# Graph attention on one core: V of a pair of tiles as seven block products in the scores' banks

## What is computed

```
q, k, v = (heads(x @ W + b) for W, b in the three pairs)      # 16 heads of 32
scores  = q k^T / sqrt(32), -inf where adj == 0
out     = softmax(scores) v  -> (b, s, 512)
x       = layernorm(x + out @ Wo + bo)       # no scale or shift, eps 1e-5
```

## Time and profile before

| | us |
|---|---|
| median of three runs | 822.24 |
| the profiled execution, whole | 821.39 |
| its span, first to last instruction | 819.5 |
| TensorE busy | 812.0 (99%) |
| VectorE busy | 544.9 (66%) |
| GpSimd busy | 512.6 (63%) |
| ScalarE busy | 238.2 (29%) |
| granted TensorE clock, mean | 0.999 |

### The profile page before, as it was taken

The page is one execution under the profiler, slowest core; times in us unless marked ns, Lnnn a source line. Parts: engine busy times, 40 slices in busy tenths (PEclk is TensorE's granted clock), DMA queues, the critical chain, the costliest instruction groups (busy, mean ns, idle before and its releaser), DMA issues.

```text
span 819.5 us, 25422 instructions
## 1 busy us (share of the span) xinstructions
PE 812.0 (99%) x11286; PEld 665.1 (81%) x11286; DVE 544.9 (66%) x691; ACT 238.2 (29%) x315; POOL 512.6 (63%) x407
## 2 busy tenths in 40 slices
PE   9999999999999999999999999999999999999997
PEld 7788888888888888888888888888888888888886
DVE  5667667766567666676665776656766567766795
ACT  6532233221332222332223322133322233223223
POOL 1386667656675565856658566576665767657682
PEclk9999999999999999999999999999999999999999
DMA  9224424253342433424334243352424434234342
GB/s 321 90 79 122 120 81 135 84 143 95 88 143 72 149 92 92 139 70 142 105 91 134 71 144 95 82 154 82 128 88 106 136 82 131 84 108 118 105 105 104
DMA packets 50173, 92.37 MB, mean 113 GB/s; under 512 B 11280, under 2 KB 13328, under 8 KB 47888
## 3 DMA queue, kind: packets, MB, share of 16 engines
q1 hardware_dynamic: 47568, 87.08, 36.2%
q10 hardware_dynamic: 2496, 3.67, 1.6%
HBM read 40.37 MB, written 16.78 MB: 70 GB/s over the span
## 4 chain that ended last, share of the span: by engine, by line
PE 98%; DVE 1%; POOL 0%; ACT 0%; issue 0%; POOLq 0%; DVEq 0%
PE ring L289 23%; PE ring L291 21%; PE ring L290 21%; PE ring L386 7%; PE ring L387 7%; PE ring L390 7%; PE psum_s L357 6%; PE ring L375 6%; PE ring L407 1%; PE ring L309 0%; POOL soft L912 0%; PE ring L313 0%; PE ring L317 0%; DVE soft L717 0%; DVE top L724 0%; ACT soft L568 0%
## 5 line engine op out<-in xcount | busy, mean ns | idle before, releaser
L912 POOL TENSOR_TENSOR soft<-soft,top 128x1024 f32<-128x1024 f32 x62 | 125.2, 2020 | 77.5 <-DVE top L724 77.5
L171 POOL TENSOR_TENSOR soft<-soft,inverse 128x1024 f32<-128x1024 f32 x62 | 118.9, 1918 | 24.9 <-DVE inverse L731 22.2
L563 ACT ACTIVATE kt<-ring,bk 128x512 f32<-128x512 f32 x64 | 43.6, 681 | 258.7 <-PE ring L291 258.6
L889 POOL TENSOR_TENSOR x_lo<-x_raw,x_hi 128x512 fp32r<-128x512 f32 x56 | 72.0, 1286 | 61.1 <-ACT x_hi L548 61.1
L289 PE MATMUL ring<-wv_hi,x_hi 128*128 128x512 f32 x256 | 103.5, 404 | 0.0
L289 PE MATMUL ring<-x_hi,wk_hi 128*128 128x512 f32 x256 | 103.1, 403 | 0.0
L728 DVE TENSOR_REDUCE total<-soft 128x16 f32<-128x1024 f32 x62 | 75.6, 1219 | 41.0 <-ACT soft L568 41.0
L291 PE MATMUL ring<-wv_hi,x_lo 128*128 128x512 f32 x256 | 100.1, 391 | 0.0
L291 PE MATMUL ring<-x_hi,wk_lo 128*128 128x512 f32 x256 | 99.9, 390 | 0.0
L290 PE MATMUL ring<-x_lo,wk_hi 128*128 128x512 f32 x256 | 99.7, 390 | 0.0
L290 PE MATMUL ring<-wv_lo,x_hi 128*128 128x512 f32 x256 | 99.6, 389 | 0.0
(11 more groups left out here) (81 smaller groups left out, 1362.3 us busy)
## 6 DMA issues: line engine op xcount, KB each, us to landing
pt<-soft SPq DMA_DIRECT2D x464, 64.0 KB, 2.0
x_raw<-in_xt SPq DMA_DIRECT2D x15, 1024.0 KB, 6.8
row<-in_x SPq DMA_DIRECT2D x60, 256.0 KB, 2.7
out_rows<-row SPq DMA_DIRECT2D x60, 256.0 KB, 2.6
adj<-in_adj SPq DMA_DIRECT2D x16, 128.0 KB, 2.9
pt<-soft ACTq DMA_DIRECT2D x32, 64.0 KB, 2.2
kt<-in_wk SPq DMA_DIRECT2D x4, 256.0 KB, 5.1
row<-in_wv SPq DMA_DIRECT2D x1, 1024.0 KB, 8.4
```

The lines of the kernel that those rows point to most:

```text
L171: ops.tensor_tensor(soft_of(c), soft_of(c), on_keys(inverse[:, c % 2, :]), ALU.mult).then_inc(normed, 1)
L889: nc.gpsimd.tensor_tensor(x_lo[:, buf, :, rows], x_raw[:, :, rows], x_hi[:, buf, :, rows].bitcast(F32), ALU.subtract).then_inc(x_lo_done, 1)
L912: nc.gpsimd.tensor_tensor(soft_of(c), soft_of(c), on_keys(top[:, c % 2, :]), ALU.subtract).then_inc(centred, 1)
```

## The change

For pairs 1 to 27, V of the pair (256 rows x 512 features times 512 x 512) is seen as 2 x 2 blocks: row block i is a tile, feature half j, column half of the weights 256 wide. Seven products of blocks take the place of eight; each is 2 chunks x 3 terms = 6 matmuls of 256 columns. Four of them need sums of input blocks, made anew for each pair: `load_pair` loads the pair's inputs a second time into the slots of `v` that V will fill, VectorE adds (`add_inputs`), ScalarE and GpSimd make hi and lo parts (`split_sums`). The sums of the weights are made once at the start, in the memory of `pt`. The products go into the four banks of the scores, between the masks of the pair and the next scores: P1, P2, P4, P5, P6 in `first_products`, after the mixing; P7 and P3 in `last_products`, between the two output projections. VectorE reads seven times (`read_first`, `read_middle`, `read_last`) and adds up in `v`.

With it: `pt` has two slots instead of four, so placing waits for the mixing of the pair before; `bias` is not repeated over the chunks, and `mask` adds it in two halves; the K and Q projections after the scores no longer wait for reads of V; on SP load_row(b) and load_pair stand ahead of place(a); on GpSimd add_bo(a) stands between centre(a) and centre(b), and add_bo(b) right behind the normalising. The diff, without the declarations of semaphores, the changed counts in the tail, and unchanged lines between:

```diff
+SEVEN = range(1, FULL)
+HALF = D // 2
+P1, P2, P4, P5, P6, P7, P3, PARTS = 1, 2, 3, 4, 5, 6, 7, 7
...
-        pt = sb("pt", [P, 4, 2, HEADS, SQ])
+        pt = sb("pt", [P, 2, 2, HEADS, SQ])
+        s_hi = sb("s_hi", [P, KC, 2 * P], F32R)
+        s_lo = sb("s_lo", [P, KC, 2 * P], F32R)
+        t_hi = sb("t_hi", [P, 4, 2, HALF], F32R)
+        t_lo = sb("t_lo", [P, 4, 2, HALF], F32R)
-        bias = sb("bias", [P, 2, GT, 2, KC, SQ])
+        bias = sb("bias", [P, 2, GT, 2, SQ])
...
+        def pt_of(c):
+            if c >= TILES - 6 and c // 2 % 2 == 1:
+                return kt[:, 0, c % 2 * 2:c % 2 * 2 + 2, :].rearrange("p q (h k) -> p q h k", k=SQ)
+            return pt[:, c % 2]
+        def pt_users(c):
+            return c - 3 if c >= TILES - 6 else c - 1
         def block_of(c, q, k):
-            return pt[to:to + SQ, c % 4, q % 2, :, :], soft_of(c)[q * SQ:(q + 1) * SQ, k, :, :]
+            return pt_of(c)[to:to + SQ, q % 2, :, :], soft_of(c)[q * SQ:(q + 1) * SQ, k, :, :]
+        def s_raw(m):
+            return v[:, 2 * m % 4:2 * m % 4 + 2, :].rearrange("p t (c n) -> p (t c) n", n=2 * P)
+        def at(rows, i, j):
+            return rows[:, 2 * j:2 * j + 2, i * P:(i + 1) * P]
+        def w_raw_block(i, j):
+            return w_raw[2][:, 2 * i:2 * i + 2, j * HALF:(j + 1) * HALF]
+        def t_raw(n):
+            return pt[:, n // 2, n % 2, :, :].rearrange("p h k -> p (h k)").rearrange("p (c n) -> p c n", c=2)
+        def s_bank(n):
+            return psum_s[:, n].rearrange("p t b c k -> p (t b c k)")
+        def first_sums():
+            return s_bank(1)[:, 0:HALF]
+        def second(n):
+            return s_bank(3 * n)[:, 0:HALF]
+        def other_sums():
+            return s_bank(2)[:, 0:HALF]
+        def v_reads(m):
+            return PARTS * (m - SEVEN.start)
...
+        def v_count(c):
+            return c + 1 if c < 2 * SEVEN.start else c + 1 - 2 * len(SEVEN)
...
             def place(c):
-                wait_for(sp, mixed, c - 3)
+                wait_for(sp, mixed, pt_users(c))
+                if c < 2:
+                    sp.wait_ge(t_lo_done, 4)
...
+            def load_pair(m):
+                wait_for(sp, mixed, 2 * m - 2)
+                G, t = 2 * m // GT, 2 * m % GT
+                sp.dma_start(s_raw(m), xt_dram[G, :, :, t * P:(t + 2) * P]).then_inc(s_in[m % 2], DMA)
...
             load_x(1)
+            sp.wait_ge(t_raw_done, 4)
             load_row(0)
+            load_pair(1)
             for p in range(FULL):
                 a, b = 2 * p, 2 * p + 1
                         load_x(p // 2 + 2)
                 if p >= 2:
                     store(a - 3)
+                load_row(b)
+                if p >= 1 and p + 1 in SEVEN:
+                    load_pair(p + 1)
                 place(a)
-                load_row(b)
                 place(b)
                 if p >= 1:
                     store(a - 2)
-                    wait_for(pe, masked, c)
+                    wait_for(pe, masked, 2 * c)
+                    if c // 2 > SEVEN.start:
+                        pe.wait_ge(v_read, v_reads(min(c // 2, SEVEN.stop)))
...
-                    pe.wait_ge(v_done, c + 2)
+                    if c // 2 in SEVEN:
+                        pe.wait_ge(v_read, v_reads(c // 2 + 1))
+                    else:
+                        pe.wait_ge(v_done, v_count(c + 1))
...
-                                                    v[own, c % 4, h * DH:(h + 1) * DH], pt[own, c % 4, :, r * KC + kc, :],
+                                                    v[own, c % 4, h * DH:(h + 1) * DH], pt_of(c)[own, :, r * KC + kc, :],
+            def product(out, left_hi, left_lo, right_hi, right_lo, adds=False):
+                for kc in range(2):
+                    nc.tensor.matmul(out, left_hi[:, kc, :], right_hi[:, kc, :], start=kc == 0 and not adds, stop=False,
+                                     skip_group_check=adds)
+                    nc.tensor.matmul(out, left_hi[:, kc, :], right_lo[:, kc, :], start=False, stop=False,
+                                     skip_group_check=adds)
+                    last = nc.tensor.matmul(out, left_lo[:, kc, :], right_hi[:, kc, :], start=False, stop=kc == 1,
+                                            skip_group_check=adds)
+                last.then_inc(v_part, 1)
+            def inputs_block(m, i, j):
+                buf, rows = 2 * m // GT % 2, slice((2 * m % GT + i) * P, (2 * m % GT + i + 1) * P)
+                return x_hi[:, buf, 2 * j:2 * j + 2, rows], x_lo[:, buf, 2 * j:2 * j + 2, rows]
+            def inputs_sum(n):
+                i, j = ((1, 1), (0, 0), (1, 0), (0, 1))[n - 1]
+                return at(s_hi, i, j), at(s_lo, i, j)
+            def weights_block(i, j):
+                columns = slice(j * HALF, (j + 1) * HALF)
+                return w_hi[2][:, 2 * i:2 * i + 2, columns], w_lo[2][:, 2 * i:2 * i + 2, columns]
+            def weights_sum(n):
+                return t_hi[:, n - 1], t_lo[:, n - 1]
+            def first_products(m):
+                pe.wait_ge(masked, 4 * (m + 1))
+                if m == SEVEN.start:
+                    pe.wait_ge(t_hi_done, 4)
+                    pe.wait_ge(t_lo_done, 4)
+                product(first_sums(), *inputs_block(m, 0, 0), *weights_block(0, 0))
+                product(second(0), *inputs_block(m, 0, 1), *weights_block(1, 0))
+                product(second(1), *inputs_block(m, 1, 1), *weights_sum(4))
+                pe.wait_ge(s_hi_done, m - SEVEN.start + 1)
+                pe.wait_ge(s_lo_done, m - SEVEN.start + 1)
+                product(other_sums(), *inputs_sum(1), *weights_sum(1))
+                pe.wait_ge(v_read, v_reads(m) + P1)
+                product(first_sums(), *inputs_sum(2), *weights_sum(2), adds=True)
+            def last_products(m):
+                pe.wait_ge(v_read, v_reads(m) + P6)
+                product(first_sums(), *inputs_sum(3), *weights_sum(3), adds=True)
+                product(other_sums(), *inputs_sum(4), *weights_block(1, 1), adds=True)
...
                 a, b = 2 * p, 2 * p + 1
                 score(a)
                 score(b)
-                pe.wait_ge(v_done, a - 1)
+                if p == 1:
+                    pe.wait_ge(v_done, 1)
+                else:
+                    pe.wait_ge(k_done, a + 4)
                 project_k(a + 4)
-                pe.wait_ge(v_done, a)
+                if p == 1:
+                    pe.wait_ge(v_done, 2)
+                else:
+                    pe.wait_ge(q_done, a + 4)
                 project_q(a + 4)
                 project_k(b + 4)
                 mix(a - 2)
                 mix(b - 2)
-                pe.wait_ge(k_done, b + 5)
-                project_v(a)
-                pe.wait_ge(q_done, b + 5)
-                project_v(b)
+                first_products(p)
                 project_out(a - 2)
+                last_products(p)
                 project_out(b - 2)
...
             project_v(T - 8)
             project_q(T - 1)
-            pe.wait_ge(v_done, T - 7)
+            pe.wait_ge(v_done, v_count(T - 7 - 1))
             project_k(T - 1)
             project_v(T - 7)
...
-                    act.wait_ge(v_proj, c - 2 * GT + 1)
+                    tile = c - 2 * GT
+                    if tile // 2 in SEVEN:
+                        act.wait_ge(v_part, v_reads(tile // 2) + (P2, P4)[tile % 2])
+                    else:
+                        act.wait_ge(v_proj, v_count(tile))
...
             def place(c):
-                wait_for(act, mixed, c - 3)
+                wait_for(act, mixed, pt_users(c))
+                if c < 2:
+                    act.wait_ge(t_lo_done, 4)
+            def split_sums(m):
+                act.wait_ge(s_raw_done, 4 * (m - SEVEN.start + 1))
+                wait_for(act, v_part, v_reads(m))
+                nc.scalar.copy(s_hi[:, :, :], s_raw(m)).then_inc(s_hi_done, 1)
+            def split_weight_sums(n):
+                act.wait_ge(t_raw_done, 4)
+                nc.scalar.copy(t_hi[:, n], t_raw(n)).then_inc(t_hi_done, 1)
...
             read_k(3)
             split_w(3, 2)
             split_w(3, 3)
+            for n in range(4):
+                split_weight_sums(n)
             for p in range(FULL):
                 a, b = 2 * p, 2 * p + 1
                         split_x(c + 2 * GT)
                         place(c)
+                if p + 1 in SEVEN:
+                    split_sums(p + 1)
...
             def read_v(c):
-                dve.wait_ge(v_proj, c + 1)
+                dve.wait_ge(v_proj, v_count(c))
+            def add_inputs(m):
+                x, done = s_raw(m), 4 * (m - SEVEN.start)
+                dve.wait_ge(s_in[m % 2], DMA * ((m - SEVEN.start) // 2 + 1))
+                nc.vector.tensor_tensor(at(x, 1, 1), at(x, 1, 0), at(x, 1, 1), ALU.add).then_inc(s_raw_done, 1)
+                dve.wait_ge(s_raw_done, done + 1)
```

(93 more changed lines are left out.)

34 lines of the change are left out of this document (19 added, 15 removed).

## The result

The changed kernel takes **817.6 us** (median of 4 runs, 816.9 to 818.1), the kernel before, measured with it, 822.05 (821.5 to 822.4): a ratio of 0.9946, with a 95% interval of 0.9928 to 0.9963. It is faster, by 4.45 us where I had forecast 8.5. The profiled execution of after took 818.06 with a span of 814.6; that of before had a span of 819.5. So the spans differ by 4.9, and on the spans the rest is worked out.

A forecast was written before the change was run, and what follows sets the result against it. TensorE, busy 99% of the span, was taken as the bound. From the median 822.24 us, -11.3 (V) + 0.8 (late rows) + 2.0 (start) = -8.5 gave 813.7 us, range 810.5 to 824.

The forecast's parts named there:

- V, 0.42 a pair: TensorE's V block: 42 half-width matmuls replace 24 full ones, gaining 0.42 us a pair, 11.3 us over 27 pairs.
- rival 3: TensorE: weight loads of the short matmuls come to light, so nothing is saved, 1029 us; chance 0.01.
- The walk: One pair's period followed engine by engine: TensorE stays continuous, period 24.75 us, about 1 us to spare.
- VectorE's sum: VectorE's work per pair: some 3.9 us added to 16.7, making 20.6 us of a 24.75 period.
- read_q, 1.1 us spare on paper: ScalarE's read of Q ends at 8.7 in the period; project_q(b+4) wants it at 9.8.
- Rival 1: Chain VectorE, GpSimd, ScalarE runs 1.3 to 1.5 us longer, taking back 0.2 to 0.35 a pair, 820.5 us; chance 0.21.
- The steady 0.8 us: Late rows hold add_bo(a) on GpSimd in some pairs: 0.03 us a pair charged, bounds 0 and 9.5 us in all.
- The start, 2.0: Start through pair 1: GpSimd's low parts +0.5, add_bo(0) +0.35, pair 1's split of sums +1.1; bounds 0.5 and 4 us.
- The tail, taken as 0 (to 0.3): After the pairs with new V: nothing new but mask halves, 0 to 0.3 us, taken as 0.
- the likeliest case: The forecast itself holds: 811 to 816.5 us, chance 0.60.
- Rival 2: SP's queue binds through a 23.9 us cycle; slower issues give 825 or 859 us; chance 0.17.

The follow-up runs named there:

- run 1: Kernel before, with only place(b) held back on SP until project_out(a-2) is through, so its DMAs run over the scores: 828.9 us, ratio 1.0077.
- run 2: Changed kernel, with ScalarE's queue issuing four of the eight DMAs of every placing so that placings end before the scores: 814.3 us, ratio 0.9903.
- run 8: Kernel before, with 8 added 64 KB copies from SBUF to SBUF over the scores of each pair, which nothing reads: 828.9 us, ratio 1.0080.
- run 7: Changed kernel with GpSimd's old order, add_bo(a) behind both normalisings and add_bo(b) behind split_x: 817.8 us, ratio 0.9941.
- run 10: Kernel with placings shared by ScalarE's queue, start reordered: weight sums split earlier, pair 0's bo additions later, pair 1's input sums made between VectorE's two sums: 814.4 us.
- run 11: The same reordered start, plus tail weights of tiles 56 and 57 placed into the memory of the input sums: 814.1 us, ratio 0.9898.
- run 12: Kernel with placings shared by ScalarE's queue, its order before the loop kept, pair 1's input sums made behind the first transpose of pair 0: 814.0 us.
- run 3: Changed kernel with both SP loads, load_row(b) and load_pair, moved behind place(a): 909.2 us, ratio 1.106.
- run 5: Changed kernel with load_pair alone moved behind place(a) on SP: 835.8 us, ratio 1.0148.
- run 6: Changed kernel with load_row(b) alone moved behind place(a) on SP: 971.4 us, ratio 1.181.

## Why the prediction was right or wrong

- **V, 0.42 a pair: right.** The block went from 5.59 to 5.12, and the separated output projections give back 0.06: 0.41. Steps of 0.120 as in the earlier trace rows; rival 3 fell.
- **The walk: right in its order and mostly to 0.3 us.** In the pair at 372.94, mask(a) at 2.4 (2.5 forecast), the split of the sums 2.40 us long (2.5), P6 read at 19.3 (19.2), transpose(a) at 13.2 (13.0). VectorE's sum was taken 0.9 us a pair too high (20.6, measured 19.7). No wait of TensorE for a read behind pair 1; read_q, 1.1 us spare on paper, was never late there. Rival 1 did not happen: the delay of 1.3 us that it needed wasn't there, and where the time came out between its 820.5 and my 813.7, it was for another reason.
- **The steady 0.8 us: the failed step.** It stood for rows that land late, and was 0: GpSimd did wait for them, but within what was spare (the waits of after: total, times, longest):

```profile
POOL row L1131 <- DMA row<-in_x: 23.1, 26, 1.9
```

The same fact, placings until 1.1 in the next period, cost 26 x 0.105 = 2.7 us by another way, which no term had: the scores themselves take longer under them. Runs 1, 2 and 8 show it from three sides. The material for it stood in the trace of before: of its 26 pairs one has scores of 1.69, and it is the one with a placing issued over most of them (SP's queue and the chain of before). I had looked at waits, and this is none.

```profile
117.63 6.34 SPq L210 DMA_DIRECT2D pt<-soft  x8
...
123.14 1.69 PE psum_s L357 x93
```

- **The start, 2.0: right in size, and its terms nearly so.** It measured 1.82 + the 0.42 of pair 1's V = 2.2. The K projection behind the first scores took 0.40 longer (forecast 0.5 for GpSimd's low parts), the Q and V projections of pair 0 together 0.38 (0.35 for add_bo(0) ahead of centre(1); run 7, without it, has them at their old length), the K and Q projections of pair 1 together 0.89 (1.1). Another 0.54 came ahead of the first scores (31.18, before 30.64), where no term stood. Runs 10 to 12 show that moving single pieces of work there doesn't shorten it; what a shorter start would take stays open.
- **The tail, taken as 0 (to 0.3): +1.1.** The scores of pair 29 took 2.13 where before they took 1.62, again under placings; with two slots of pt they wait for the mixing of the pair before:

```profile
734.99 7.11 SPq L274 DMA_DIRECT2D pt<-soft  x8
...
741.15 2.20 PE L433 MATMUL psum_s<-kt,qt 32*64 32x64 f32 x128
```

The two rows are of after, SP's queue and TensorE. These scores are 0.5 of the 1.1. The rest is in the mixing of pair 29, 2.27 instead of 1.60, in one wait ahead of its 126th matmul, with 16 placings issued over it:

```profile
778.91 1.45 PE L454 MATMUL ring<-kt,v 64*32 64x64 f32 x125
780.95 0.30 PE L454 MATMUL ring<-kt,v 64*32 64x64 f32 x3 [0.59 <-issue]
```

This wait is why runs 10 and 11 gained little or nothing: their scores there take 1.53 and 1.56, but this mixing 2.55, and the tail stays at 92.9 and 93.4. What the 126th matmul waits for, the traces don't show.
- **The sum.** -11.3 + 0.8 + 2.0 became, for the span, -11.1 (27 x 0.41) + 2.7 (scores) + 2.2 (start) + 1.1 (tail) = -5.1; measured -4.9. The time stood inside the range, but above the 816.5 that the likeliest case allowed, in the part kept for rival 1, which didn't happen. That the range held is luck of its width: the gain was about half of the forecast, by a path that no rival named.
- **Rival 2** (SP's queue): the queue never bound, at 24.88, but runs 3, 5 and 6 show how near it is: the load one place further back costs 18 us, the row 154.

## What to carry to other kernels

Where a transfer ends matters even if nobody waits for it: look at what runs over TensorE's small matmuls, not only at the waits. Here it paid to give a burst of copies within SBUF to two queues, so that it ended before them. A delay is to be compared with what is spare only if it isn't part of a loop; if the late thing delays the next issue of itself, the loop's length is what counts. And before moving a VectorE operation into a gap, see whether GpSimd works in SBUF there.
